# Experts of a mixture over all tokens, against tokens sorted by expert through memory, the steps of fixed places first and of extra places last

## The chip, the core and the metric

The kernel runs on one core of one Trainium2 chip. The metric is the time of one execution on the device in microseconds (us). Three executions of the kernel before took 678.14, 679.23 and 679.41 us; their median is 679.23. The engines are TensorE (PE, with its weight loads as PEld), VectorE (DVE), ScalarE (ACT), GpSimd (POOL) and SyncE (SP), which here only issues transfers. Each of them works through its own queue in the order in which the program wrote it.

## What is computed

The input `x` is 4 batches of 512 tokens with 128 numbers each. Two layers follow:

```
xn = _layernorm(x)
x = x + L0_attn(xn) + L0_ffn(xn)
xn = _layernorm(x)
x = x + L1_attn(xn) + L1_ffn(xn)
```

`L0_attn` is an attention between the channels of 16 heads. `L0_ffn` is the part that changes: a router picks 8 of 64 experts for each token, and each expert is a small gated network with 88 hidden numbers; a shared one of 176 hidden numbers takes every token.

```
expert_out = jax.vmap(lambda gw_, uw_, dw_: _mlp(x, gw_, uw_, dw_))(Wg, Wu, Wd)
routed = jnp.einsum('eth,te->th', expert_out, rw)
shared = _mlp(x, Sg, Su, Sd)
```

Here `_mlp` is `silu(x @ gw.T) * (x @ uw.T) @ dw.T`, and `rw` holds a token's weight for each expert, which is zero for 56 of the 64. `L1_attn` compares each token with the 64 before it, by head, and keeps the 32 nearest of them; `L1_ffn` is a network with ternary weights and 512 hidden numbers. Everything is float32.

## The kernel before

All tokens of a batch stay in SBUF, and every expert is computed for every token; the weights `rw` then remove what was not chosen. The hidden rows of all experts stand behind one another: 2 x 88 shared rows and 64 x 88 routed rows make `NF` = 46 tiles of 128 rows for each batch, so 4 x 46 = 184 steps. A step `n` does this:

- ACT rounds a tile of the weights to float32r (`highs`, tile `Whi`), and POOL takes the remainder (`splits`, tile `Wlo`).
- PE multiplies by the tokens in three products for the gate and three for the up part (`experts`, banks G and U), each 512 columns wide: high by high, high by low, low by high.
- ACT takes the silu (`silus`), DVE multiplies gate and up (`products`, tile S). The routing weights are multiplied in on POOL (`tiles`, `S<-S,Rb`) or on DVE (`weights`, `S<-Rb,bank_G`). To have them by hidden row, PE spreads the router's table with a 0/1 matrix (`spread`).
- PE adds the tile's part of the output into bank A with a float32 matmul of 512 columns (`downs`); the trace has two records for such a matmul.

Only the three small steps of routing (`route`: scores, the best 4 of 8 groups, the best 8 experts), the channel attention (`attend`) and the second layer (`head`, `distances`, `choose`, `gather`, `dense_up`, `dense_down`) stand beside that. `choose` is the selection of the nearest 32: for each of the 8 groups `g` of a batch, DVE runs four rounds of MAX8 and MATCH_REPLACE8 on four tiles.

The order of all this isn't left to a scheduler. Each engine's parts are generators, and `weave` calls them letter by letter from a string in the table `ORDER`; waits between engines are semaphores that the parts set themselves. SP loads all weights once, in about 45 us, and later only stores the output. All these lines are recorded through helpers, so L522, L859, L1345 and L1654 are the lines of the helpers of PE, DVE, ACT and POOL. `S` is a ring of five tiles; free tiles of the second layer (`hf`, `wT` and others) take its place early on.

## Time and profile before

| | us |
|---|---|
| three executions, median | 679.23 |
| the profiled execution, span of its instructions | 676.3 |
| PE busy in it | 638.7 |
| DVE busy | 545.1 |
| ACT busy | 444.6 |
| POOL busy | 365.4 |
| data moved by transfers | 15.81 MB |

The span runs from the first to the last instruction; the 2.9 us between it and the median lie around it, and no row shows them. Busy time is that in which an engine had at least one instruction under way. A matmul's record ends when its last column is through, and the next one starts before that, so the cost of a matmul in a full queue is read from start to start. Issuing a transfer doesn't count as busy; on SP it has a row of its own (SPq).

### The profile page before, as it was taken

The numbers are of one execution on the slowest core, as the hardware profiler recorded it, in microseconds if no ns is written. First come the engines' busy times: TensorE is split into PE (matmuls) and PEld (weight loads), VectorE is DVE, ScalarE is ACT, GpSimd is POOL, SyncE is SP. The second block draws the span as 40 slices with busy tenths as digits, with TensorE's granted clock in tenths as the row PEclk, the third lists the DMA queues.
The fourth block names the chain that finished last, engine by engine and source line by source line (L and its number), as shares of the span: only waits on it lengthen the run. The fifth ranks groups of instructions, "written<-read, shape, count | busy, mean of one in ns | idle before, by whom it ended". The sixth has DMA issues, their size and how long they took to land.

```text
span 676.3 us, 14256 instructions
## 1 busy us (share of the span) xinstructions
PE 638.7 (94%) x4792; PEld 430.7 (64%) x4792; DVE 545.1 (81%) x2461; ACT 444.6 (66%) x802; POOL 365.4 (54%) x448
## 2 busy tenths in 40 slices
PE   4887999999999999999999999999999999998886
PEld 3544766667656666767567567666567776675675
DVE  5987778645975999997976899965485999967997
ACT  3674454646787957448587786455888956467953
POOL 2278366566462787665452886653763576621220
PEclk9999999999999999999999999999999999999999
DMA  8940000000000000000000000000000000000000
GB/s 297 392 131 1 0 1 0 1 0 1 0 1 1 2 2 1 1 1 1 2 0 2 2 1 2 1 1 1 1 1 1 2 1 1 1 1 17 18 18 17
DMA packets 12968, 15.81 MB, mean 23 GB/s; under 512 B 1728, under 2 KB 10832, under 8 KB 12384
## 3 DMA queue, kind: packets, MB, share of 16 engines
q1 hardware_dynamic: 12896, 14.91, 6.3%
q8 instruction: 38, 0.62, 0.4%
q14 instruction: 34, 0.28, 0.1%
HBM read 13.85 MB, written 1.05 MB: 22 GB/s over the span
## 4 chain that ended last, share of the span: by engine, by line
PE 61%; DVE 24%; ACT 7%; POOL 4%; issue 3%; DMA 0%; DVEq 0%; POOLq 0%; ACTq 0%
PE bank_A L522 17%; PE bank_U L522 14%; PE bank_G L522 14%; PE bank_X L522 14%; DVE Wk L1278 6%; DVE m L1275 5%; DVE S L859 4%; DVE GWk L859 2%; POOL PR L1654 2%; ACT L1350 1%; PE bank_X L531 1%; ACT Ed L1345 1%; PE bank_X L825 1%; ACT PR L1345 1%; ACT L1345 1%
## 5 line engine op out<-in xcount | busy, mean ns | idle before, releaser
L1654 POOL TENSOR_TENSOR Wlo<-Wgu,Whi 128x256 fp32r<-128x256 f32 x184 | 134.9, 743 | 119.5 <-ACT Whi L1345 116.5
L522 PE MATMUL bank_A<-S,WdT 128*128 128x512 f32 x346 | 172.2, 599 | 0.2 <-POOL S L1654 0.2
L1654 POOL TENSOR_TENSOR S<-S,Rb 128x512 f32<-128x512 f32 x84 | 108.6, 1294 | 72.0 <-DVE S L859 71.4
L859 DVE TENSOR_TENSOR S<-S,bank_U 128x512 f32<-128x512 f32 x173 | 116.6, 684 | 37.5 <-PE bank_U L522 23.3
L1345 ACT ACTIVATE Whi<-Wgu 128x256 fp32r<-128x256 f32 x184 | 73.0, 413 | 53.0 <-PE bank_U L522 48.5
L522 PE MATMUL bank_G<-xH,Whi 128*128 128x512 f32 x184 | 94.7, 515 | 8.0 <-POOL Wlo L1654 3.8
L522 PE MATMUL bank_U<-xH,Whi 128*128 128x512 f32 x184 | 93.4, 508 | 1.6 <-DVE wT L859 1.1
L522 PEld LDWEIGHTS bank_A<-S,WdT 128*128 128x128 f32 x346 | 61.7, 189 | 34.6 <-issue 21.4
L1278 DVE MATCH_REPLACE8 Wk<-m,Wk 128x79 f32<-128x79 f32 x384 | 82.2, 226 | 0.0
L1345 ACT ACTIVATE bank_G<-bank_G 128x512 f32<-128x512 f32 x83 | 48.4, 583 | 42.9 <-PE bank_G L522 42.6
L1345 ACT ACTIVATE S<-bank_G 128x512 f32<-128x512 f32 x90 | 53.7, 596 | 34.3 <-PE bank_G L522 27.5
L859 DVE TENSOR_TENSOR S<-Rb,bank_G 128x512 f32<-128x512 f32 x83 | 56.4, 680 | 22.5 <-ACT bank_G L1345 17.6
L522 PE MATMUL bank_U<-xH,Wlo 128*128 128x512 f32 x184 | 72.9, 396 | 0.0
L522 PE MATMUL bank_G<-xH,Wlo 128*128 128x512 f32 x184 | 72.9, 396 | 0.0
L522 PE MATMUL bank_G<-xL,Whi 128*128 128x512 f32 x184 | 72.8, 396 | 0.0
L522 PE MATMUL bank_U<-xL,Whi 128*128 128x512 f32 x184 | 72.7, 395 | 0.0
L1275 DVE MAX8 m<-Wk 128x8 f32<-128x79 f32 x384 | 63.9, 228 | 0.0
L522 PEld LDWEIGHTS bank_G<-xH,Whi 128*128 128x128 f32 x184 | 34.7, 189 | 34.7 <-issue 17.2
L522 PEld LDWEIGHTS bank_U<-xH,Whi 128*128 128x128 f32 x184 | 34.7, 189 | 23.8 <-issue 8.9
L1345 ACT ACT_TABLE_LOAD x38 | 48.8, 1283 | 0.7
L1350 ACT ACT_TABLE_LOAD x35 | 44.9, 1283 | 6.5 <-DVE mv L926 4.4
L1654 POOL TENSOR_TENSOR Wk<-Ed,Wk 128x316 f32<-128x316 f32 x31 | 26.8, 863 | 37.1 <-DVE Wk L1278 36.9
(294 smaller groups left out, 1176.0 us busy)
## 6 DMA issues: line engine op xcount, KB each, us to landing
Wgu<-in_Wgu SPq DMA_DIRECT2D x2, 2048.0 KB, 14.4
xs<-in_x SPq DMA_DIRECT2D x4, 256.0 KB, 6.0
wqk<-in_w_qkv SPq DMA_DIRECT2D x1, 1024.0 KB, 6.9
Wgu<-in_Wgu SPq DMA_DIRECT2D x1, 1024.0 KB, 9.5
out<-xs SPq DMA_DIRECT2D x3, 256.0 KB, 2.3
Wgu<-in_Wgu SPq DMA_DIRECT2D x1, 512.0 KB, 4.7
wout<-in_w_out SPq DMA_DIRECT2D x1, 512.0 KB, 8.1
wvT<-in_wvT SPq DMA_DIRECT2D x1, 512.0 KB, 9.2
```

The lines of the kernel that those rows point to most:

```text
L522: return engine.matmul(dst, lhsT, rhs, start=start, stop=stop)
L531: p = engine.transpose(t[0:rows, 128 * i:128 * i + 128], src3[:, i, :], ident)
L825: p = engine.transpose(t[:, 128 * i:128 * i + 128], Wm[s][:, i, :], ident)
L859: return engine.tensor_tensor(dst, a, b, op)
L1275: top[i] = own(engine.max(w8[:, i, 8 * r:8 * r + 8], v[:, i, :]))
L1278: p = engine.match_replace(wk[:, i, :], w8[:, i, 8 * r:8 * r + 8], v[:, i, :], TAKEN)
L1345: return engine.activation(dst, src, f, bias=bias, scale=scale, accum_out=acc)
L1350: engine.preload_act_table_set(LNEXP)
L1654: return engine.tensor_tensor(dst, a, b, op)
```

## The change

The routed experts are no longer computed for all tokens. A batch's tokens are sorted by expert through two tables in HBM, `XS` (inputs) and `YS` (results), each in two copies for even and odd batches.

- Places. Each expert has 64 fixed places (`SLOT`), so 4,096 rows of the table. Tokens beyond the 64th of an expert go to further blocks of 64 places, up to 64 such blocks, the second half of the table. DVE and PE work out each token's place from running counts (bank `rank`, three more PE parts and some 60 more DVE instructions in `route`, 32 of them small ones for the weight of each token's choice) and write it as `rows`; which expert an extra block belongs to goes into `erow`.
- Sending. POOL issues 32 indirect transfers per batch (`sends`), each of which writes 128 tokens of 512 bytes to their places. The tables of inputs are cleared first by two transfers of 4 MB from a zero tile.
- Steps. A batch has 18 steps: 2 shared ones on all tokens, then 16 routed ones of 8 blocks of 64 places. The first 8 routed steps take the fixed places, the last 8 the extra ones, whether these are filled or not. For a routed step, SP loads 512 rows of `XS` (`slots_in`), PE transposes them (4 transposes, `slot_turns`), runs 8 float32 matmuls of 176 columns with 64 stationary columns each, gate and up together (`experts`), ACT takes 2 silus, DVE 2 products of 176 columns, PE transposes back (4, `hidden_turns`), ACT copies, PE runs 8 float32 matmuls of 128 columns (`downs`), ACT copies, SP stores 256 KB to `YS` (`slots_out`).
- Weights. Those of 60 experts stay in SBUF (`WE`, 152 KB each as [128, 304]). Those of 4 more for the fixed places, and those of every extra block, come through a ring of 16 (`RING`), two steps deep: 272 loads of 152 KB, 42 MB in all. The address of an extra block's weights is read from `erow` into registers of SP, four at a time.
- Fetching back. When all 16 steps of a batch are stored, POOL issues 32 indirect reads (`gets`) of 128 rows into a ring of 8 tiles (`LAND`), and DVE adds each to the tokens with its weight (`joins`, 128 in all).
- Gone are the float32r split (`highs`, `splits`), the weights on hidden tiles (`tiles`, `weights`), the spreading (`spread`, `RW`, `Rb`), and the sum through `mo`.
- The table `ORDER` is new for all engines. Products of experts are now float32 throughout.

```diff
-NF = 46
-NR = 44
+SHARED = 2
+QUADS = 16
+STEPS = SHARED + QUADS
+SLOT = 64
+GUD = 2 * NI + C
+ROWS = 2 * NE * SLOT
+KEY = 2.0 ** -14
+RES = 60
+RING = 16
+LAND = 8
...
-        Wgu = sb("Wgu", [128, NF, 256])
-        Whi = [sb(f"Whi{i}", [128, 256], FR) for i in range(WRING)]
-        Wlo = [sb(f"Wlo{i}", [128, 256], FR) for i in range(WRING)]
-        WdT = sb("WdT", [128, NF, 128])
+        WE = sb("WE", [128, RES, GUD])
+        Wr = sb("Wr", [128, RING, GUD])
+        SW = sb("SW", [128, SHARED, 2 * NI])
+        SD = sb("SD", [NI, SHARED, C])
...
+def spill(n):
+
+    return routed(n) % QUADS >= QUADS // 2
+
+
+def quad(n):
+
+    return routed(n) % (QUADS // 2)
+
+
+def slots_of(n):
+
+    return (ROWS // 2 if spill(n) else 0) + 8 * SLOT * quad(n)
...
+            def clear(r):
+
+                sp.wait_ge("zeroed", 1)
+                z4 = Wm[0][:, :, :].rearrange("p a c -> p (a c)").unsqueeze(1).to_broadcast([128, ROWS // 512, 512])
+                load(f"cleared{r}", XS[r].rearrange("(p a r) c -> p a (r c)", p=128, r=4), z4)
...
+            def slots_in():
+                for m in range(B * QUADS):
+                    n = step_of(m)
+                    b = n // STEPS
+                    yield
+                    sp.wait_ge(*scattered(b))
+                    if m >= 2:
+                        sp.wait_ge(full(bank("xt", step_of(m - 2))), nth("xt", step_of(m - 2)) + 1)
+                    load(loaded(m)[0], xq[m % 2][:, :, :],
+                         XS[b % 2][slots_of(n):slots_of(n) + 512, :].rearrange("(j p) c -> p j c", p=128))
+
+            def slots_out():
+                for m in range(B * QUADS):
+                    n = step_of(m)
+                    b = n // STEPS
+                    yield
+                    sp.wait_ge(empty(bank("y", n)), nth("y", n) + 1)
+                    if b >= 2:
+                        sp.wait_ge("joined_y", NT * 8 * (b - 1))
+                    load(f"st_y{m % 2}", YS[b % 2][slots_of(n):slots_of(n) + 512, :].rearrange("(j p) c -> p j c", p=128),
+                         yq[m % 2][:, :, :])
+
+            def weights():
+                owner = list(stream)
+                at = {}
+                for k, (n, t) in enumerate(owner):
+                    b = n // STEPS
+                    yield
+                    e = 8 * quad(n) + t
+                    if k >= RING:
+                        sp.wait_ge("down", owner[k - RING][0] + 1)
+                    if spill(n):
+                        if t % 4 == 0:
+                            sp.wait_ge(empty(bank("rank", b)), nth("rank", b) + 1)
+                            _, at = nc.values_load_multi_w_load_instructions(
+                                erow[0:1, b, e:e + 4], engines=[engine.engine], min_val=0, max_val=(NE - 1) * C,
+                                skip_runtime_bounds_check_because="a count of at most 63 experts, times 128")
+                        src = d["WE"][bass.ds(at[t % 4], C), :]
+                    else:
+                        src = d["WE"][e * C:(e + 1) * C, :]
+                    load(f"ld_r{k % RING}", Wr[:, k % RING, :], src)
...
+            def slot_turns():
+                for m in range(B * QUADS):
+                    n = step_of(m)
+                    yield
+                    t = fill("xt", n)
+                    pe.wait_ge("ld_c", 16)
+                    pe.wait_ge(*loaded(m))
+                    turn4(t, xq[m % 2]).then_inc(sems(full(bank("xt", n))), 1)
+
             def experts():
                 for n in range(total):
-                    b, j, w = n // NF, n % NF, n % WRING
-                    xH, xL = xHs[b % 2], xLs[b % 2]
-                    for key, at in (("g", 0), ("u", 128)):
+                    b, s = n // STEPS, n % STEPS
+                    for k, key in enumerate("gu"):
                         yield
                         t = fill(key, n)
-                        if j == 0:
-                            pe.wait_ge("xL" if b else "xL0", b if b else 1)
-                        pe.wait_ge("wlo", n + 1)
-                        mm(t[:, :], Whi[w][:, at:at + 128], xH[:, :], True, False)
-                        mm(t[:, :], Whi[w][:, at:at + 128], xL[:, :], False, False)
-                        mm(t[:, :], Wlo[w][:, at:at + 128], xH[:, :], False, True).then_inc(
-                            sems(full(bank(key, n))), 1)
+                        if shared(n):
+                            pe.wait_ge(empty(bank("xT", b)), nth("xT", b) + 1)
+                            pe.wait_ge("ld_s", 32)
+                            for i in range(2):
+                                at = 128 * (2 * k + i)
+                                p = mm(t[:, 2 * NI * i:2 * NI * (i + 1)], xTs[b % 2][:, at:at + 128], SW[:, s, :])
+                        else:
+                            pe.wait_ge(empty(bank("xt", n)), nth("xt", n) + 1)
+                            for i in range(2):
+                                for h in range(2):
+                                    at, w = 128 * (2 * k + i) + SLOT * h, 2 * (2 * k + i) + h
+                                    weight_here(pe, n, w)
+                                    p = mm(t[SLOT * h:SLOT * (h + 1), 2 * NI * i:2 * NI * (i + 1)],
+                                           xqT[routed(n) % 2][:, at:at + SLOT], weight(n, w)[:, 0:2 * NI])
+                        p.then_inc(sems(full(bank(key, n))), 1)
...
                     else:
-                        pe.wait_ge(empty(bank("u", m)), nth("u", m) + 1)
-                    mm(T_["A"][:, :], WdT[:, m % NF, :], product_tile(m), m % NF == 0, m % NF == NF - 1).then_inc(
-                        sems("down"), 1)
+                        t = fill("y", n)
+                        pe.wait_ge(empty(bank("ht", n)), nth("ht", n) + 1)
+                        for w in range(8):
+                            i, h = w // 2, w % 2
+                            weight_here(pe, n, w)
+                            p = mm(t[SLOT * h:SLOT * (h + 1), 128 * i:128 * i + 128], hT[:, SLOT * w:SLOT * (w + 1)],
+                                   weight(n, w)[0:NI, 2 * NI:])
+                    p.then_inc(sems("down"), 1)
...
+                t = fill("rank", b)
+                pe.wait_ge("before", 1)
+                pe.wait_ge("marks", b + 1)
+                for j in range(NT):
+                    for i in range(j + 1):
+                        mm(t[:, NE * j:NE * j + NE], before[:, 128:] if i == j else before[:, 0:128],
+                           marks[:, NE * i:NE * i + NE], i == 0, i == j)
+                for i in range(NT):
+                    p = mm(t[0:NE, 320:322], marks[:, NE * i:NE * i + NE], before[:, 0:2], i == 0, i == NT - 1)
+                p.then_inc(sems(full(bank("rank", b))), 1)
+                yield
+                pe.wait_ge("ove", b + 1)
+                mm(ps("rank", b)[:, 384:448], K("ones", NE), ovE[:, :]).then_inc(sems("ovb"), 1)
+                yield
+                pe.wait_ge("ej", b + 1)
+                mm(ps("rank", b)[0:1, 448:512], rk[:, 3:4], ident[0:NE, 0:NE]).then_inc(sems("erow"), 1)
...
             def products():
                 for n in range(total):
-                    s = product_tile(n)
-                    yield
-                    dve.wait_ge(empty(bank("g", n)), nth("g", n) + 1)
-                    t = filled("u", n)
-                    emptied(tt(s, s, t[:, :], ALU.mult), "u", n)
...
+                    for k, key in enumerate("gu"):
                         yield
+                        dve.wait_ge("silu", 2 * n + k + 1)
+                        if n:
+                            dve.wait_ge(full(bank("ht", n - 1)), nth("ht", n - 1) + 1)
+                        t = filled(key, n)
+                        u = t[:, 0:4 * NI].rearrange("p (j w) -> p j w", j=2)[:, :, NI:]
+                        emptied(tt(hs[:, 2 * k:2 * k + 2, :], sg[:, 2 * k:2 * k + 2, :], u, ALU.mult), key, n)
...
+            def joins():
+                for b in range(B):
+                    for q in range(NT * 8):
+                        n, i, k = b * NT * 8 + q, q % NT, q // NT
+                        yield
+                        if q < NT:
+                            dve.wait_ge(empty(bank("ysh", b)), nth("ysh", b) + 1)
+                            dve.wait_ge("wsel", b + 1)
+                        else:
+                            dve.wait_ge("joined_y", n - NT + 1)
+                        dve.wait_ge(f"got{n % LAND}", 16 * (n // LAND + 1))
+                        x = xb(b)[:, i, :]
+                        stt(x, land[:, n % LAND, :], wsel[:, b, i, k:k + 1], x, ALU.mult, ALU.add).then_inc(
+                            sems("joined_y"), 1)
...
-            def split(n):
-                w = n % WRING
-                po.wait_ge("whi", n + 1)
-                tt(Wlo[w][:, :], Wgu[:, n % NF, :], Whi[w][:, :].bitcast(F), ALU.subtract).then_inc(sems("wlo"), 1)
...
+            def sends():
+                for b in range(B):
+                    r = b % 2
+                    for k in range(8):
+                        for i in range(NT):
+                            yield
+                            po.wait_ge("rows", b + 1)
+                            po.wait_ge(f"cleared{r}", 16)
+                            if b >= 2:
+                                for q in range(2):
+                                    po.wait_ge(f"ld_x_{q}", 16 * (QUADS // 2) * (b - 1))
+                            at = 8 * i + k
+                            engine.indirect_dma_start(
+                                out=XS[r], out_offset=bass.IndirectOffsetOnAxis(ap=rows[:, b, at:at + 1], axis=0),
+                                in_=xns[r][:, i, :], in_offset=None).then_inc(sems(scattered(b)[0]), 16)
+
+            def gets():
+                for b in range(B):
+                    for q in range(NT * 8):
+                        n, at = b * NT * 8 + q, 8 * (q % NT) + q // NT
                         yield
-                        s, k = product_tile(n), (n % NF - (NF - NR)) // BLOCK
-                        po.wait_ge(empty(bank("sp", n // NF, k)), nth("sp", n // NF, k) + 1)
-                        po.wait_ge(empty(bank("u", n)), nth("u", n) + 1)
-                        tt(s, s, Rb[k][:, :], ALU.mult).then_inc(sems("tw_p"), 1)
+                        for k in range(2):
+                            po.wait_ge(*stored(k, b))
+                        if n >= LAND:
+                            po.wait_ge("joined_y", n - LAND + 1)
+                        engine.indirect_dma_start(
+                            out=land[:, n % LAND, :], out_offset=None, in_=YS[b % 2],
+                            in_offset=bass.IndirectOffsetOnAxis(ap=rows[:, b, at:at + 1], axis=0)).then_inc(
+                            sems(f"got{n % LAND}"), 16)```

Three places show what the new table and the new parts do to the queues. The first is POOL. Before, a stretch of its queue in the steps of a middle batch, up to where that batch's channel attention (tiles `PR` and `z`) comes in:

```order
L1654 TENSOR_TENSOR S<-S,Rb 128x512 [waits U1_emptied]
L1654 TENSOR_TENSOR Wlo<-Wgu,Whi 128x256 [waits whi] x2
L1654 TENSOR_TENSOR S<-S,Rb 128x512 [waits U1_emptied]
L1654 TENSOR_TENSOR Wlo<-Wgu,Whi 128x256 [waits whi]
L1654 TENSOR_TENSOR PR<-GWk,wqk 128x256 [waits X0_filled,X0_emptied]
```

Now, the same engine from its first sends (`XS<-xn,rows`, batch 0) on; the `PR` and `z` rows are batch 0's attention:

```order
L1810 DMA XS<-xn,rows 8192x128 [waits cleared0,rows]
L1810 DMA XS<-xn,rows 8192x128 x4
L1792 TENSOR_TENSOR PR<-GWk,wqk 128x256 [waits X1_filled,X1_emptied]
L1792 TENSOR_TENSOR PR<-GWk,wqk 128x256 x3
L1810 DMA XS<-xn,rows 8192x128 x3
L1792 TENSOR_TENSOR PR<-PR 128x512 [waits k0]
L1810 DMA XS<-xn,rows 8192x128 [waits pool]
L1810 DMA XS<-xn,rows 8192x128 x2
L1792 TENSOR_TENSOR PR<-PR,z 128x512
```

The attention that batch 0's sends share the queue with is behind or between them; all 32 sends of a batch stand ahead of its first routed step. In the whole queue the order is: sends of batch 0, of batch 1, fetches of batch 0, sends of batch 2, then the sends of batch 3 mixed with the fetches of batch 1 and the second layer of batch 0, and last the fetches of batches 2 and 3.

The second place is SP among the extra steps of batch 0. Before, SP had nothing there: its 42 rows are the loads at the start and the stores of the output. Now (`TENSOR_LOAD erow` reads four addresses, `Wr` is the ring of weights, `ISA` is register work for an address):

```order
L489 DMA YS<-yq 128x4x128 [waits A_emptied]
L489 DMA xq<-XS 128x4x128 [waits U0_filled]
L578 TENSOR_LOAD erow [waits down]
L489 ISA
L489 DMA Wr<-in_WE 128x304
L489 ISA
L489 DMA Wr<-in_WE 128x304
L489 DMA YS<-yq 128x4x128 [waits A_emptied]
L489 ISA
L489 DMA Wr<-in_WE 128x304
L489 ISA
L489 DMA Wr<-in_WE 128x304
```

For each extra step SP now issues 8 loads of weights, a load and a store of places, and 2 reads of addresses, 12 things in one queue, and each waits for what stands ahead of it.

The third place is DVE behind the last product of the last expert step. Before, the last product of batch 3 (`S<-S,bank_U`) had 8 groups of `choose` behind it or next to it; now, after the last product (`hs<-sg,bank_G`), 16 groups follow, those of batch 2 with the joins of batch 3 (`xs<-land,wsel,xs`) between them, then those of batch 3. A piece of it, in the groups of batch 2:

```order
L1421 MAX m<-Wk 128x8 [waits dve] x4
L1424 MATCH_REPLACE Wk<-m,Wk 128x79 [waits dve] x4
L981 SCALAR_TENSOR_TENSOR xs<-land,wsel,xs 128x128 [waits got6,joined_y]
L981 SCALAR_TENSOR_TENSOR xs<-land,wsel,xs 128x128 [waits got7,joined_y]
L1433 TENSOR_REDUCE sm<-m 128x4
L1434 RECIPROCAL sm<-sm 128x4 [waits dve]
L981 SCALAR_TENSOR_TENSOR xs<-land,wsel,xs 128x128 [waits got0,joined_y]
```

So the second layer of batch 2 has moved behind the experts of batch 3.

## Rows read from the trace of the kernel before

**Rows 1.** The page's span and part 1; a window: busy us (count) PE, PEld, DVE, ACT, POOL.

```profile
span 676.3 us, 14256 instructions
...
PE 638.7 (94%) x4792; PEld 430.7 (64%) x4792; DVE 545.1 (81%) x2461; ACT 444.6 (66%) x802; POOL 365.4 (54%) x448
...
90.00:600.00 510.00, 504.26 (x3557) 333.06 (x3556) 418.50 (x1840) 342.07 (x611) 306.56 (x374) 1.00 0.01 1
```

**Rows 2.** Timeline of PE (start, length, instruction), then the chain that ended last.

```profile
138.11 0.39 PE L522 MATMUL bank_G<-xH,Wlo 128*128 128x512 f32 x1
138.34 0.40 PE L522 MATMUL bank_U<-xH,Whi 128*128 128x512 f32 x1
...
139.20 1.72 PE bank_A L522 x4
```

**Rows 3.** Groups by form, POOL: count, busy us, mean ns, idle time before.

```profile
L1654 POOL TENSOR_TENSOR Wlo<-Wgu,Whi 128x256 fp32r<-128x256 f32 x184 | 134.9, 743 | 119.5 <-ACT Whi L1345 116.5 <-DVE hg L867 2.6
L1654 POOL TENSOR_TENSOR S<-S,Rb 128x512 f32<-128x512 f32 x84 | 108.6, 1294 | 72.0 <-DVE S L859 71.4
```

**Rows 4.** The same for DVE.

```profile
L859 DVE TENSOR_TENSOR S<-S,bank_U 128x512 f32<-128x512 f32 x173 | 116.6, 684 | 37.5 <-PE bank_U L522 23.3 <-ACT S L1345 12.1
...
L859 DVE TENSOR_TENSOR S<-Rb,bank_G 128x512 f32<-128x512 f32 x83 | 56.4, 680 | 22.5 <-ACT bank_G L1345 17.6 <-PE bank_A L522 4.8
```

**Rows 5.** The same for ACT.

```profile
L1345 ACT ACTIVATE Whi<-Wgu 128x256 fp32r<-128x256 f32 x184 | 73.0, 413 | 53.0 <-PE bank_U L522 48.5 <-DMA WdT<-in_WdT 1.3
L1345 ACT ACTIVATE S<-bank_G 128x512 f32<-128x512 f32 x90 | 53.7, 596 | 34.3 <-PE bank_G L522 27.5 <-PE bank_A L522 6.4
```

**Rows 6.** Timeline of PE: small float32 matmuls and the row behind each.

```profile
70.02 1.95 PE L522 MATMUL bank_X<-PR,wvT 128*128 128x128 f32 x16
71.81 0.39 PE L522 MATMUL bank_X<-cst,Qb 128*128 128x128 f32 x2
...
242.34 0.60 PE L825 MATMUL bank_X<-cst,Wm 128*128 128x128 f32 x4
242.70 0.48 PE L522 MATMUL bank_G<-xH,Whi 128*128 128x512 f32 x1
...
273.84 1.09 PE L522 MATMUL bank_X<-wout,z 64*64 64x128 f32 x16
274.86 0.50 PE L522 MATMUL bank_G<-xH,Whi 128*128 128x512 f32 x1
```

**Rows 7.** Timeline of SP's issues at the start.

```profile
39.15 0.42 SPq L450 DMA_DIRECT2D hbu<-in_Vb  x1
39.61 0.42 SPq L450 DMA_DIRECT2D dec<-in_dec  x1
```

**Rows 8.** Windows at the start (clock, DMA share, GB/s last); transfers with us to landing.

```profile
20.00:25.00 5.00, 4.78 (x16) 2.59 (x15) 4.60 (x12) 2.43 (x5) 1.49 (x3) 1.00 0.99 417
...
out<-xs SPq DMA_DIRECT2D x3, 256.0 KB, 2.3
...
out<-xs SPq DMA_DIRECT2D x4, 64.0 KB, 1.5
```

**Rows 9.** DVE at the start; POOL on tile PR in a window; POOL.

```profile
26.19 0.21 DVE L1059 MATCH_REPLACE8 wk<-m8r,sfc 128x64 f32<-128x64 f32 x1
...
37.90 1.77 DVE L859 TENSOR_TENSOR yT<-yT,Rb 128x512 f32<-128x512 f32 x1
...
33.00:59.00 26.00, 7.88 (x8) 1.00 0.32 98
...
57.25 1.05 POOL L1654 TENSOR_TENSOR z<-z,rq 128x512 f32<-128x512 f32 x1
```

**Rows 10.** Timeline of DVE, two groups of a selection; the window of the end.

```profile
620.36 0.67 DVE L1275 MAX8 m<-Ed 128x8 f32<-128x79 f32 x4 [2.59 <-ACT Ed L1345]
...
626.40 0.66 DVE L1275 MAX8 m<-Ed 128x8 f32<-128x79 f32 x4
...
600.70:676.30 75.60, 61.55 (x889) 49.04 (x888) 60.58 (x445) 51.80 (x103) 14.24 (x18) 0.96 0.05 16
```

643 lines of the change are left out of this document (322 added, 321 removed).

## The prediction, written before the result

> **What bounds the kernel now.** I read the busy times and a long window first. PE is busy for 638.7 us of the 676.3, and from 90 to 600 us for 504 of 510 [rows 1]; DVE, ACT and POOL have room. So the kernel before is bound by PE's instruction stream up to about 600 us, and then by something else. The timeline of PE gives the price of a step: the float32r products of 512 columns start 0.23 us apart, and two float32 matmuls of the output take 1.72 us, 0.86 each [rows 2]. A step costs 6 x 0.23 + 0.86 = 2.25 us, and 184 of them 414 us. All other work on PE is 638.7 - 414 = 225 us. The last 75.6 us are the second layer of batch 3, from its layer norm on: in it DVE works for 60.6 us, and its selection goes at 6.04 us per group of four tiles, 8 groups in a batch [rows 10].
>
> **What the change does to each engine's total.** *PE.* Four transposes take 0.36 us from their start to the next row's, 0.09 each. Eight matmuls of 128 columns on part of the array (`wout,z`) take 1.02 us, 0.13 each, while on the whole array eight take 1.79 us, 0.22 each [rows 6]. The new matmuls have 64 stationary columns and alternate between the two halves of the bank's partitions, as `wout,z` does, so I take 0.13 for 128 columns and 0.13 x 176/128 = 0.175 for 176. The other end is the whole array's price, 0.22 and 0.31. A routed step is 8 x 0.09 + 8 x 0.175 + 8 x 0.13 = 3.15 us, at most 4.9; 64 of them are 202 us. A shared step is 4 x 0.31 + 4 x 0.09 + 4 x 0.22 = 2.5 us, 8 of them 20. The ranks of routing cost PE about what the spreading did. The sum is 225 + 202 + 20 = 447 us, 190 less than before; with the dear price, 560.
>
> *DVE* loses the products and weights of 512 columns, 116.6 + 56.4 us in the two large groups and some 15 in smaller ones [rows 4]. It gains 144 products of 176 columns (0.68 x 176/512 = 0.24, I take 0.3 with what a short instruction costs; 43 us), 128 joins of 128 columns at 0.25 by the same scaling (0.17 and what a short instruction costs; 32 us), and about 10 us per batch of routing. 545 - 188 + 43 + 32 + 40 = 472 us. *ACT* loses the 73.0 us of `Whi` and about 110 us of silus of 512 columns (184 at 0.6), and gains per routed step three copies of 512 columns at 0.6 and two short silus, 2.4 us [rows 5]: 444.6 - 183 + 64 x 2.4 + 10 = 425 us. *POOL* loses 134.9 and 108.6 [rows 3] and about 16 smaller ones, which leaves 106 us, and gains 256 indirect transfers at a price P that no row of this trace shows. *SP* goes from 42 rows to 734.
>
> So no engine is full any more by its total, and what decides is the chain: places of batch 0, its sends, four batches of steps, the end.
>
> **The chain, stage by stage.** (a) *Places of batch 0.* Now the best 8 are marked at 26.4 us [rows 9]. Counting, ranks and places add some 20 small instructions and four changes of engine, about 7 us: 33 us.
>
> (b) *Sends.* All 32 stand ahead of the first load of places, and batch 0's attention stands between them on POOL: 7.9 us on `PR` and three more of 1.05 [rows 9], 11 us. P is bounded from below by what SP needs for an issue, 0.47 us from start to start [rows 7], and from above by 2.3 us, the landing of 256 KB; 64 KB landed in 1.5 [rows 8]. A send has a list to read and 128 rows to write, so it should be nearer to the landing of the same 64 KB than to a plain issue; I take 1.2. 32 x 1.2 + 11 + 2.3 for the first load, and 1.5 of `xl`: 53 us, so the first routed step begins near 86 us. In the order, PE has until then only routing, attention and shared steps, some 45 us of its 225.
>
> By the Trainium skill, "DMA: Bandwidth & Descriptors", section "Anatomy of one DMA — SWDGE (gpsimd) path", a GpSimd transfer costs about 2.0 us, of which most is the receipt of the last write and little is the making of descriptors. By it POOL would be held much shorter than 1.2 us; were it held for SP's 0.47 [rows 7], this stage would be 23 us shorter and the time 608. No run here shows a transfer from GpSimd.
>
> (c) *A batch of 16 steps.* PE's other work is 225 less the 45 ahead, 62 in the last 75.6 us [rows 10], and about 30 for the second layer of batch 2, which the new order puts behind the experts: 88 us, 22 per batch. The fixed half is bound by PE: 8 x 3.15 + 2 x 2.5 + 11 = 41 us. The extra half isn't. There SP issues 10 transfers per step, 10 x 0.47 = 4.7 us [rows 7], and two reads of addresses. Such a read is in no row; it can cost nothing beside an issue, or as much as a small transfer's 1.5 us [rows 8]; I take 1 us, so SP needs 6.7 us. The ring holds only two steps, and a step's weights can be asked for only when the step two before has finished, which hides none of the landings; I add 0.8 and take 7.5 us per extra step. The transfers themselves fit: 1.25 MB of weights, 0.5 of places and about 0.3 of sends or fetches are 2 MB, at the 417 GB/s of the start [rows 8] 5 us. So the extra half is 60 us, a batch 101, four 404 us. The bounds: with SP free, PE sets 41 + 36 = 77 us per batch, 308 in all; with 1.5 us per read and no overlap of the landing (2.3), 10 us per step and 121 per batch.
>
> Hidden under that, with its price if the cover goes: POOL must run 192 sends and fetches, 68 us of attention and second layer, from 33 us until batch 3's sends are done, 33 + 192 x 1.2 + 68 = 331 us, while batch 3's steps are due at 86 + 303 = 389. The cover is 58 us, gone at P = 1.5.
>
> (d) *The end.* Behind the last product stand the second layers of batches 2 and 3. Batch 2: 8 x 6.04 for its groups, 32 joins of batch 3 (8 us), and its `gather` 6 us, together 62. The fetches of batch 3 go meanwhile: 32 x 1.2 and 14 us for the groups' weights, 52, hidden. Then batch 3's second layer as now, 75.6. Together 138 us.
>
> The sum is 86 + 404 + 138 = 628 us of span. The profiled span of before is 676.3, and the median 679.23 lies 2.9 above it; so the time is **631 us**, 7% faster.
>
> **Rivals.** *A: POOL is the bound, and it is slower.* Each 0.1 us on P above 1.2 adds 3.2 us in (b), above 1.5 also 19 in (c), and above 1.5 about 3 in (d). For 48 us more (to 679): 0.3 x 32 = 10, then 38 at 25 per 0.1, so the point is P = 1.65; at P = 1.9 the time is 631 + 10 + 4 x 25, about 741. For it speaks that DVE and POOL already hold each other up: a DVE product of two tiles in SBUF took 1.77 us [rows 9] where one with an operand in a bank takes 0.68 [rows 4], and sends write while DVE is busy. Against it: POOL has no data to work through in a send. The Trainium skill, "SBUF — State Buffer", section "Who interferes with whom", says that DVE's two-port copies lock GpSimd out so that it cannot write descriptors; that rule makes P larger than it is alone, and this rival likelier. Chance 0.15.
>
> *B: the extra steps cost over 9 us each, and it is slower.* They are 32; 48 us more is 1.5 us each, 9.0 in place of 7.5. A read of addresses of 1.7 us does it, or the landing of each step's weights in the open, as in the upper bound of (c): 631 + 80 = 711. For it: the ring of two steps, and one queue in which loads of places wait behind loads of weights. Against it: transfers have landed while others were issued in the start. Chance 0.15.
>
> *C: SP hides behind PE.* Reads are near nothing, issues overlap PE's work: 308 us for the batches in place of 404, so 535 in all; half of the way, 583. Chance 0.15. *D: the gain on PE is eaten by matmuls at the whole array's price*, 1.7 us more in each fixed step (in the extra ones SP still covers it), 54 us: 685, a little slower. Chance 0.04, with the pairs in [rows 6] against it.
>
> **Numbers.** My forecast, 600 to 665 us, has 0.51. Faster by over 0.2% (less than which a measurement of this kernel can't tell from no change): 0.51 + C 0.15 + a share of A, B and D that stays under 678, 0.02: 0.68. Same 0.02. Slower 0.30. The range that holds 8 in 10 leaves out the best of C and the worst of A and B: 570 to 715 us; the forecast's own range is 600 to 665.
>
> **What the profile would show.** PE busy near 450 us. The first load of `xq` near 84 us, and `XS<-xn` issues on POOL 1.2 us apart. Extra steps 7.5 us apart with PE waiting for `Wr`, SP's queue full in them; fixed steps 5 us apart. The last product (`hs`) near 490 us, and 138 us behind it in which DVE is busy. The prediction is wrong if POOL's queue is full from 33 us to the end (A), if extra steps come over 9 us apart (B), or under 6 (C).

## The result, and the profile after

On the first occasion the changed kernel took 823.12 us (median of 4 runs, 821.74 to 825.49) against 679.32 us of before: 1.2109 times as long, interval 1.2078 to 1.214. I had predicted 631, with a range of 570 to 715. The page of that execution, and the answers to [rows 3 to 5] (this and all further groups: line, engine, output and input, count, then busy us, mean ns, and the idle time before):

```profile
span 821.1 us, 18063 instructions
...
PE 605.7 (74%) x6064; PEld 446.5 (54%) x6064; DVE 475.8 (58%) x2788; ACT 379.2 (46%) x728; POOL 361.6 (44%) x405
...
PEclk9995656988979976976689877789959998756985
...
L1810 POOL DMA_INDIRECT XS<-xn,rows x128 | 126.4, 988 | 75.5 <-issue 43.5
L1823 POOL DMA_INDIRECT land<-YS,rows x128 | 123.8, 967 | 77.5 <-issue 40.5
L973 DVE TENSOR_TENSOR hs<-sg,bank_G 128x176 f32<-128x176 f32 x144 | 47.1, 333 | 127.8 <-ACT sg L1493 54.1
```

No engine is full, as expected, and DVE (472 expected) and POOL (106 and 256 transfers) are where the sums had them; ACT is 46 us under its 425. PE is 159 us above its 447, at a mean granted clock of 0.807 where before had 0.996.

The same kernel, unchanged, took 818.02 us on a second occasion and **683.67 us on a third** (677.54 to 690.74, 5 runs; before 679.17 beside it; ratio 1.0027, interval 0.9945 to 1.0108). Six near copies of it, below, lie between 684.63 and 690.64 us. The kernel before, too, has one slow execution on record, 906.92 us at a mean clock of 0.66, among 25 with a median of 679.24. So two things have to be explained: some 139 us (823 less 684) that came with the occasion, and the 53 us between 631 and 684. The page of the third occasion, then the windows between its stages (first the first routed step of batch 0, then the beginning of its extra half, and so on to the last product; columns as in [rows 8]: length, busy us of PE, its weight loads, DVE, ACT, POOL, then clock, DMA share, GB/s):

```profile
span 681.9 us, 18063 instructions
...
PE 540.6 (79%) x6064; PEld 401.2 (59%) x6064; DVE 478.1 (70%) x2788; ACT 380.5 (56%) x728; POOL 361.0 (53%) x405
```

```profile
0.00:105.60 105.60, 63.84 (x275) 45.54 (x275) 60.84 (x294) 18.05 (x31) 52.14 (x63) 0.85 0.74 250
105.60:132.20 26.60, 25.82 (x278) 19.77 (x278) 14.41 (x75) 18.11 (x37) 17.75 (x18) 0.88 0.73 215
132.20:194.40 62.20, 59.62 (x579) 43.84 (x577) 37.14 (x135) 37.52 (x74) 32.47 (x36) 1.00 0.83 241
194.40:239.60 45.20, 40.12 (x361) 30.78 (x360) 32.34 (x158) 23.59 (x49) 30.90 (x36) 0.92 0.51 143
239.60:310.90 71.30, 60.49 (x661) 43.52 (x660) 45.40 (x238) 47.76 (x94) 48.96 (x50) 0.95 0.77 225
310.90:348.80 37.90, 36.23 (x524) 28.44 (x522) 30.05 (x196) 30.03 (x58) 26.79 (x31) 1.00 0.63 181
348.80:427.40 78.60, 61.55 (x731) 43.50 (x729) 49.46 (x285) 53.59 (x97) 46.59 (x52) 0.89 0.74 214
427.40:467.40 40.00, 37.65 (x570) 30.15 (x568) 38.12 (x253) 32.70 (x65) 25.68 (x29) 1.00 0.61 170
467.40:528.30 60.90, 50.94 (x643) 35.38 (x642) 45.93 (x261) 43.00 (x81) 21.05 (x26) 0.97 0.79 225
528.30:606.00 77.70, 53.36 (x771) 43.66 (x769) 65.94 (x467) 39.25 (x70) 45.12 (x53) 0.76 0.16 43
606.00:681.90 75.90, 51.02 (x696) 36.60 (x695) 58.49 (x436) 36.86 (x78) 13.56 (x17) 0.75 0.03 8
```

Added up, with the same cuts in the first trace (115.8, 152.7, 225.2, 278.5, 377.6, 434.7, 532.9, 581, 650 us), in us:

| stage | predicted | first occasion | third |
|---|---|---|---|
| up to the first routed step | 86 | 115.8 | 105.6 |
| four fixed halves | 164 | 195.4 | 149.7 |
| four extra halves | 240 | 338.8 | 273.0 |
| behind the last product | 138 | 171.1 | 153.6 |
| span | 628 | 821.1 | 681.9 |

In the eight windows of the batches of the third occasion PE is busy for 372 of 422.7 us, 88%. There it is the engine nearest to full, as before the change (99%, [rows 1]).

### The profile page after: what moved, and what is told of

Its sections match the earlier page's. It is cut to its first block and busy times, and to the rows that moved or that the text cites. A ratio compares the mean times of both kernels' runs of the same rounds, so it can differ in the third digit from the quotient of the medians.

```text
span 821.1 us, 18063 instructions
## 1 busy us (share of the span) xinstructions
PE 605.7 (74%) x6064; PEld 446.5 (54%) x6064; DVE 475.8 (58%) x2788; ACT 379.2 (46%) x728; POOL 361.6 (44%) x405
## 5 line engine op out<-in xcount | busy, mean ns | idle before, releaser
L1810 POOL DMA_INDIRECT XS<-xn,rows x128 | 126.4, 988 | 75.5 <-issue 43.5
L1823 POOL DMA_INDIRECT land<-YS,rows x128 | 123.8, 967 | 77.5 <-issue 40.5
L973 DVE TENSOR_TENSOR hs<-sg,bank_G 128x176 f32<-128x176 f32 x144 | 47.1, 333 | 127.8 <-ACT sg L1493 54.1
L1493 ACT ACTIVATE sg<-bank_G 128x176 f32<-128x176 f32 x144 | 44.9, 317 | 95.7 <-PE bank_G L612 54.6
L1424 DVE MATCH_REPLACE8 Wk<-m,Wk 128x79 f32<-128x79 f32 x384 | 82.4, 228 | 0.0
L612 PE MATMUL bank_G<-Wr,xqT 128*64 128x176 f32 x544 | 76.0, 370 | 7.0 <-issue 4.2
L1792 POOL TENSOR_TENSOR Wk<-Ed,Wk 128x316 f32<-128x316 f32 x31 | 26.8, 863 | 95.0 <-DVE Wk L1424 94.3
L1493 ACT ACTIVATE hT<-bank_U 88x512 f32<-88x512 f32 x72 | 42.6, 591 | 55.4 <-PE bank_U L621 28.0
L1421 DVE MAX8 m<-Wk 128x8 f32<-128x79 f32 x384 | 64.1, 229 | 0.5 <-DVE m L1421 0.5
L621 PE MATMUL bank_U<-cst,xq 128*128 128x128 f32 x256 | 50.9, 333 | 16.8 <-DMA xq<-XS 8.9
L612 PE MATMUL bank_A<-Wr,hT 88*64 88x128 f32 x544 | 50.4, 327 | 13.6 <-ACT hT L1493 6.2
L612 PEld LDWEIGHTS bank_G<-Wr,xqT 128*64 128x64 f32 x544 | 44.0, 157 | 29.9 <-issue 17.7
L612 PE MATMUL bank_G<-WE,xqT 128*64 128x176 f32 x480 | 55.3, 361 | 6.6 <-DVE hs L973 4.2
L621 PE MATMUL bank_U<-cst,hs 128*88 128x128 f32 x288 | 52.6, 313 | 9.4 <-DVE hs L973 8.8
L1493 ACT ACTIVATE yq<-bank_A 128x512 f32<-128x512 f32 x64 | 38.1, 595 | 41.0 <-PE bank_A L612 22.4
L1493 ACT ACTIVATE xqT<-bank_U 128x512 f32<-128x512 f32 x64 | 38.1, 595 | 38.1 <-PE bank_U L621 22.2
L621 PEld LDWEIGHTS bank_U<-cst,xq 128*128 128x128 f32 x256 | 35.7, 169 | 30.8 <-issue 23.3
L612 PEld LDWEIGHTS bank_A<-Wr,hT 88*64 88x64 f32 x544 | 38.8, 165 | 24.4 <-issue 21.3
L621 PEld LDWEIGHTS bank_U<-cst,hs 128*88 128x88 f32 x288 | 33.5, 138 | 25.2 <-issue 17.7
L612 PE MATMUL bank_A<-WE,hT 88*64 88x128 f32 x480 | 36.6, 290 | 12.6 <-ACT hT L1493 8.9
L612 PEld LDWEIGHTS bank_G<-WE,xqT 128*64 128x64 f32 x480 | 35.2, 154 | 19.7 <-issue 11.5
L981 DVE SCALAR_TENSOR_TENSOR xs<-land,wsel,xs 128x128 f32<-128x128 f32 x128 | 44.9, 379 | 0.3 <-DMA land<-YS,rows 0.2
## 6 DMA issues: line engine op xcount, KB each, us to landing
xq<-XS SPq DMA_DIRECT2D x64, 256.0 KB
YS<-yq SPq DMA_DIRECT2D x64, 256.0 KB
xs<-in_x SPq DMA_DIRECT2D x4, 256.0 KB, 11.4
```

The lines of the kernel that those rows point to most:

```text
L612: return engine.matmul(dst, lhsT, rhs, start=start, stop=stop)
L621: p = engine.transpose(t[0:rows, 128 * i:128 * i + 128], src3[:, i, :], ident)
L973: return engine.tensor_tensor(dst, a, b, op)
L981: return engine.scalar_tensor_tensor(dst, a, s, b, op0, op1, accum_out=acc)
L1421: top[i] = own(engine.max(w8[:, i, 8 * r:8 * r + 8], v[:, i, :]))
L1424: p = engine.match_replace(wk[:, i, :], w8[:, i, 8 * r:8 * r + 8], v[:, i, :], TAKEN)
```

## Experiments 1: 139 us that belong to the occasion

In the first trace I saw stretches like this one. PE's timeline (start, length, instruction, in brackets the idle time before it and its releaser), POOL's, and ACT's:

```profile
347.17 0.34 PE L612 MATMUL bank_X<-mk,wqk 32*32 32x79 f32 x4 [0.28 <-issue]
348.60 0.30 PE L612 MATMUL bank_X<-mk,wqk 32*32 32x79 f32 x3 [1.08 <-issue]
350.05 0.34 PE L612 MATMUL bank_X<-mk,wqk 32*32 32x79 f32 x3 [1.16 <-issue]
...
357.43 1.27 PE L612 MATMUL bank_X<-mk,wqk 32*32 32x79 f32 x32
```

```profile
347.66 0.96 POOL L1810 DMA_INDIRECT XS<-xn,rows  x1 [0.31 <-issue]
348.93 0.96 POOL L1810 DMA_INDIRECT XS<-xn,rows  x1 [0.30 <-issue]
...
352.72 0.96 POOL L1810 DMA_INDIRECT XS<-xn,rows  x1 [0.30 <-issue]
```

```profile
347.57 0.46 ACT L1493 ACTIVATE Ra<-Pk 16x316 fp32r<-16x316 f32 x1
355.76 0.60 ACT L1493 ACTIVATE yq<-bank_A 128x512 f32<-128x512 f32 x1 [7.73 <-remote]
```

The 32 small matmuls of one group of distances took 1.27 us at 357.4 and over 9 us at 346.4, some three at a time with up to 1.2 us between them, and nothing in the program for them to wait for. Meanwhile POOL sent back to back. ACT waited too: the record of the product that fills its input in `bank_A` ends at 346.2 (1.09 us from 345.07), but that product's semaphore rises at 355.74, and ACT starts at 355.76. Over the trace PE has 53.7 us of such idle time ("issue"), 46 of them in pauses that overlap an indirect transfer of POOL; ACT has 28 us of it and 110 of waits for which the trace shows no releaser, DVE 38 and 52. I call them standstills. On the second occasion they are there again: PE 53.9 us in 64 pauses where the first had 61, and 38 of the first's 53.7 us lie within four instructions of a pause of the second. On the third PE has none, ACT 1.1, DVE 4.2.

Two more things set the first two traces apart from the third, both counted in their records of semaphores. A semaphore that a PE instruction raises does so 0.015 us behind the instruction's end (median of all three); 0.5 to 15 us behind it rose 123 and 115 times on the first two occasions, 4 times on the third. So signals came late as well, and waits without a releaser, such as ACT's above, can be waits for such a signal. And records are missing: 9,978 and 10,079 rises are recorded, 14,712 on the third. The transfers themselves took no longer: those of SP filled the DMA engines for 40.7% of 821.1 us and 48.9% of 681.9, 334 and 333 us, and those that load instructions for 0.5% and 0.7%, 4 and 5 us.

**Three variants that I first read wrongly.** Before I ran the kernel again, I had run three variants (their results stand in the next sections), and all were far under 823 us and without standstills on PE. I took this for the effect of their edits, then repeated the changed kernel.

> The changed kernel once more, unchanged, on the chip on which the runs to be compared with it run. In its first trace PE, ACT and DVE stand still for some 54, 27 and 38 us with nothing to wait for, PE always beside an indirect transfer of POOL, and 160 us of waits on ACT and DVE have no releaser in the trace; in the three variants run so far (same transfers on POOL in two of them) PE has less than 1 us of such time. If the program itself does this, the time is again 823 us and the standstills are there. If it was the chip or the run, the time is lower, 730 to 760 us, and the gains of the first three variants were too large by as much.

818.02 us, with the standstills. So it seemed to be the program itself, and I asked how little of a change removes them. With 16 matmuls of 256 columns added in the first two routed steps:

> As e2, but with filler in the first two routed steps only: 16 matmuls, 2 us of PE in all, and the rest of the program as in the changed kernel, moved by 16 instructions. If the standstills of the changed kernel belong to its logic, they are still there and the time is 815 to 825 us. If they belong to the image of the program (any shift of it changes them), they can be gone: then the time is that of the change without them, somewhere from 720 to 770 us, and the gains of the other variants have to be counted from there.

690.64 us, none. Then one PE instruction (its edit follows), one POOL instruction, one tensor in memory with a store into it at the very end, one DVE instruction:

```diff
+                    if m == 0:
+                        pe.wait_ge("before", 1)
+                        mm(t[0:2, 0:2], before[:, 0:2], before[:, 0:2])
```

> The changed kernel with one PE instruction more (a float32r matmul of 2 by 2 ahead of the first routed step). If the standstills hang on where PE's instructions lie, they vanish and the time is 685 to 700 us, as with 16 added matmuls; if they hang on another engine's or on memory, it stays at 815 to 825 us.

> The changed kernel with one POOL instruction more (a part of a tile of zeros set once before, at 10 us, ahead of all transfers), PE's, ACT's and DVE's programs untouched. If the standstills hang on POOL's program, they vanish, 685 to 700 us; if on PE's alone, 815 to 825 us.

> The changed kernel with a spare tensor of 64 KB in memory declared ahead of the places and results, and one store into it at the very end of SP's program. It moves the scratch tensors in memory and no instruction ahead of the end. If the standstills come from where the sends write, they change: any time from 685 to 825 us. If they hang on the instructions of the engines alone, 815 to 825 us.

> The changed kernel with one DVE instruction more (a small copy done twice at the start), PE's, ACT's and POOL's programs untouched. If any shift of the image does, 685 to 700 us; if only PE's or POOL's own, 815 to 825 us.

688.12, 684.63, 684.63 and 686.56 us; ratios to before 1.0135, 1.0063, 1.0086 and 1.0075, each within 0.005. All four can't be the cure, which left the suspicion that it was none of them. So the kernel itself and a copy that differs in one constant ran on one chip:

> The changed kernel unchanged, for the third time. If the standstills belong to its image, 815 to 825 us again; if they belonged to the chips of the first two occasions, 680 to 700 us like all variants with one instruction more.

> The changed kernel with one constant changed (the 1e-20 that guards a sum of weights against zero is 2e-20): the same instructions in the same places. If the standstills hang on the layout of the image, it is as slow as the changed kernel; if 680 to 700 us beside a changed kernel of 820, not even the layout is the cause.

683.67 and 685.56 us. That settles it: neither the logic of the change nor the layout of its program is enough to make the standstills, since the same program runs with them and without. What does is open. The chip of the second occasion was another one than those of the third and of all variants of the changed kernel. It ran the kernel before in its usual 678.86 us. It also ran b1 below, whose 128 indirect transfers start 3.2 us apart (median), with 0.2 us of standstill on PE. But b1 has the other two signs in small: 17 of PE's rises in its batches come 0.5 to 1.4 us late, and some 300 of about 6,870 records are missing, while b2 and b3 on the same chip, without indirect transfers, show neither. So the signs go with POOL's indirect transfers on that chip. What holds the engines up, the chip, the moment, or the recording of the profile itself (every execution has a clock on record, and where engines stood still records were lost), no run tells apart.

How 54 us become 139: PE's busy time is 605.7 against 540.6, 65 more, for the same 6064 instructions at a clock of 0.807 in place of 0.892; its standstills are 54 and 0; the rest of its idle time (waits for DVE, ACT, DMA and POOL, in which their standstills and late signals lie) is 161.7 and 141.3. 65 + 54 + 20 = 139, all that lies between the spans. Which of the 65 are the clock alone, no run shows.

## Experiments 2: PE's clock

A clock of 0.81 is a cost in itself, and it could have come from PE's pauses. So I filled them.

```diff
+            def warm(t, count):
+                for _ in range(count):
+                    mm(t[:, 0:256], before[:, 0:128], before[:, :])
...
                     t = fill("xt", n)
+                    pe.wait_ge("before", 1)
+                    warm(t, WARM)
                     pe.wait_ge("ld_c", 16)
```

> The changed kernel with idle work added on PE: ahead of each wait for places, for gate and up inputs and for hidden values of a routed step, two float32r matmuls of 256 columns into the bank that the step overwrites next, 8 per step, 512 in all, 0.11 us each at the full clock, 56 us of PE. If PE's clock (0.81 on the average, against 1.00 before) is what the change costs, and it falls because PE now stands still so often, the granted clock rises to over 0.9 in the batches, PE's own rows shorten, and the time falls to 760 to 800 us. If the clock has another cause, or PE's busy time isn't on the path, it is slower, up to 823 + 56 = 880 us.

> As the run with 512 float32r matmuls of 256 columns (e2), but each has 2 stationary and 2 moving columns: as many instructions in the same places, next to no work. e2 took the time from 818 to 734 us and also took away PE's 54 us of standstill beside POOL's transfers, so it doesn't tell the two apart. If the gain came from the work that kept PE's clock up (0.81 to 0.88), it is gone here: 810 us or more. If it came from the standstills, which depend on where the instructions lie in the program and not on what they do, PE has again almost none and the time is 710 to 760 us, with the clock near 0.81.

733.91 us with the wide filler, clock 0.884; 701.01 with the narrow one, clock 0.907; without any, 684 and 0.892. Against 823 the filler looked like a gain of 89 us; against the right base it costs 50, about its own 56 us, and the clock didn't rise. The 512 empty instructions cost 17, the work in the others 33 more. The windows say why little was to be had: in the batches the clock was already 0.88 to 1.00, and it is low where PE hardly matters, 0.75 in the last 75.9 us, which are as long as the 75.6 of before at 0.96 [rows 10]. What the wide filler does show is who bounds the batches: with 56 us more of work for PE in the routed steps they took 476.6 us in place of 421.8.

## Experiments 3: the stream of weights, and POOL's transfers

```diff
-            return WE[:, 8 * quad(n) + t, :]
+            return WE[:, min(8 * quad(n) + t, RES - 1), :]
```

(and the loads of the extra steps skipped in SP's queue)

> The changed kernel without the streaming of weights in the extra halves: the 8 extra steps of a batch multiply with the resident weights of the step with the same number in the fixed half, so tokens beyond an expert's 64 places get another expert's matrices. 256 loads of 76 KB and the 64 reads of addresses on SP are gone; every step, send, fetch and product stays. If the extra half is bound by SP and its ring of two steps, as the prediction had it, the extra steps fall from 8.5, 12.3, 11.4 and 7.8 us (in the four batches) to the 5 to 6.7 us of the fixed ones, 32 x 4.5 = 145 us less, 680 us. If they are bound by PE at its lower clock and by engines that wait for each other in the written order, little changes, less than 40 us: 785 us or more.

```diff
                         for i in range(NT):
                             yield
+                            if k >= KEEP:
+                                continue
```

(and the same for fetches and joins)

> The changed kernel with only the first four of a token's eight experts sent, fetched and joined: 64 sends and 64 fetches on POOL and 64 joins on DVE less; all steps still run, on half empty places, so the output lacks half of the experts' shares. POOL has 128 x 1.28 = 164 us less to do. If POOL's queue and what its indirect transfers do to the other engines bound the kernel, the first step starts 20 us earlier (98 in place of 116 us) and the time falls by 60 us or more. If PE, the clock and the written order bound it, the start gains at most 20 us and the rest little: 795 us or more. In the trace, all of PE's 54 us of idle time ahead of which nothing is to be waited for lie beside an indirect transfer; if these cause them, they halve to some 27 us.

676.31 and 675.69 us; against 684, some 8 us each. Both numbers hit what the expectation gave to "SP" or "POOL bounds it", for the wrong reason: the 139 us of the occasion were in the base. (The loads that e1 leaves out are of 152 KB each, not 76.) The windows of e1 answer the question by themselves. Its four extra halves, with no weight streamed:

```profile
135.20:196.30 61.10, 58.11 (x578) 44.33 (x576) 35.25 (x129) 37.35 (x74) 31.87 (x36) 0.94 0.36 107
...
243.00:307.30 64.30, 55.48 (x660) 42.24 (x658) 44.23 (x231) 47.41 (x93) 47.05 (x48) 0.95 0.39 113
...
344.60:419.10 74.50, 58.20 (x732) 41.82 (x729) 49.58 (x285) 53.42 (x97) 46.84 (x52) 0.91 0.38 108
...
456.20:518.00 61.80, 51.68 (x663) 37.47 (x662) 47.94 (x286) 42.29 (x82) 25.33 (x30) 0.92 0.34 94
```

61.1, 64.3, 74.5 and 61.8, where the kernel with the stream has 62.2, 71.3, 78.6 and 60.9: 11 us less in all. PE is busy for 223 of their 262 us.

The stages of e3 say where its 8 us come from. With 16 sends per batch the first load of places goes out 20.7 us earlier (96.11 in the changed kernel), and the first routed step starts no earlier (105.59). SP, then PE:

```profile
75.42 0.93 SPq L490 DMA_DIRECT2D xq<-XS  x2
```

```profile
106.18 1.11 PE L622 MATMUL bank_U<-cst,xq 128*128 128x128 f32 x4
```

From there to the last product it is 420.7 us against 421.8, and behind it 147.7 against 154.5. So half of the transfers gained nothing at the start or in the batches; the gain lies behind the last product, where the joins stand in DVE's queue.

> The variant with resident weights in the extra halves (e1) and the one with four of eight experts sent, fetched and joined (e3) in one kernel; the output lacks the same as theirs together. Each alone took the time from 684 to 676 us. If SP's stream and POOL's transfers covered for each other, both gone give far more than 16 us, down to 600 to 640. If PE, at a mean clock of 0.89, and the chain of four engines in the written order bound it, 655 to 672 us.

661.4 us (657.87 to 664.94). Twice 8 would have been 668, no further off than the two runs lie apart, so it isn't shown that the two cover for each other. PE with the order around it keeps the rest, as the second case said.

On the kernel before, which is bound by PE and has no routing through memory, the price of a transfer can be seen by itself:

```diff
                     split(n)
+                    if 40 <= n < 168:
+                        po.wait_ge("rows", 1)
+                        engine.indirect_dma_start(
+                            out=XS[n % 8], out_offset=bass.IndirectOffsetOnAxis(ap=rows[:, 0:1], axis=0),
+                            in_=cst[:, 0:128], in_offset=None).then_inc(sems(f"extra{n % 8}"), 16)
```

> The kernel before with 128 indirect transfers added on POOL, one behind each second half of weights of steps 40 to 167: 128 rows of 512 bytes from SBUF to a scratch tensor in memory, like the sends of the changed kernel, read by nobody. POOL gets 128 x 1.28 = 164 us more work and had 311 us of room. If an indirect transfer keeps PE from issuing (54 us beside 256 transfers, 0.2 us each, or up to 1 us in the worst stretches), the PE-bound kernel gets slower by 27 us or more beyond what the busy POOL of its sister run b2 costs; if not, it is within 5 us of it.

> The kernel before with the same amount of work on POOL in the same places, but as arithmetic: two additions of 256 columns, some 0.65 us each, in place of each of the 128 indirect transfers. It shows what POOL's lateness alone costs: from nothing to 20 us, if the ring of split weights can't cover 1.3 us at each step.

> The kernel before with the same 128 transfers of 64 KB into memory issued by SP as plain transfers at the same points. If the movement of data as such (not POOL's part in it) disturbed the other engines, it would be slower here too; expected is no change, 679 us within 3.

733.61, 780.99 and 679.31 us. POOL's groups in b1 and b2:

```profile
L1679 POOL DMA_INDIRECT XS<-cst,rows x128 | 129.8, 1014 | 20.6 <-issue 18.9
```

```profile
L1656 POOL TENSOR_TENSOR busy<-cst 128x256 f32<-128x256 f32 x256 | 189.4, 740 | 10.0
```

The data themselves cost nothing (b3). What costs is the time POOL is held: 150 us in b1 for 55 us more, 199 in b2 for 102. My first case for b1, slower than b2, is refuted, and so is my price for b2, at most 20 us. POOL's 54% of before [rows 1] wasn't room that could be filled: the `Wlo` products and the tiles of `S` stand in the same queue, and in b2 PE waits 12.9 and 17.9 us for them. Its pauses also go with a lower clock, 0.952 in place of 0.996: 37 of b2's 102 us are PE's own rows, 675.7 against 638.7.

## Experiments 4: the written order

> The changed kernel with one thing else in POOL's order: the 32 sends of batch 0 stand ahead of all pieces of its attention, where 5 of them stood ahead of the first. The sends then end near 29.4 + 32 x 1.28 = 71 us in place of 95, and the attention of batch 0 waits for that, 33 us later than now. If the start is bound by POOL's queue, the first routed step begins earlier than its 105.6 us and the time falls by up to 20 us. If it is bound by PE's order, in which the attention of batch 0 and parts of that of batch 1 stand ahead of the first routed step, that step begins later, 120 to 140 us, and the time rises by 10 to 30 us.

725.38 us. The sends end earlier and the first load of places goes out at 80.3 us in place of 96.1, but PE waits 44 us for the first piece of the attention, and its first routed step comes last in that row. SP, then PE:

```profile
80.29 0.93 SPq L489 DMA_DIRECT2D xq<-XS  x2
```

```profile
81.92 1.98 PE L612 MATMUL bank_X<-PR,cst 128*64 128x512 f32 x4 [44.38 <-POOL PR L1792]
...
144.76 1.11 PE L621 MATMUL bank_U<-cst,xq 128*128 128x128 f32 x4
```

39 us later at the first routed step (105.6 in the changed kernel) are 39 us more in the span (681.9 to 721.0). That is more than the 10 to 30 expected. Nothing later takes it up, and the start is bound by the attention that stands ahead of that step in PE's order: delaying that attention costs (n8), and halving the sends gains nothing (e3).

> The changed kernel with the same pieces of work on every engine in another written order, made by taking at each free moment of an engine the most urgent piece whose inputs are there, by the durations in the trace; one wait is added (the first dense layer behind the last attention, since both use PR). Nothing is removed: all sends, fetches, streamed weights and clears stay. If what the change costs is transfers, SP and POOL themselves, little changes: 780 us or more. If it is that engines wait for each other in the written order (DVE, ACT and POOL are busy for 58, 46 and 44% only), it takes 60 to 140 us off: 680 to 760 us.

764.08 us, without standstills, with the kernel of e7 at 690.64 on the same chip. So 73 us worse, and the second case is refuted in its sign: an order made from the durations of one trace is no better than the one written. That the order matters is shown by it, and by n8; a better one wasn't found.

## Why the prediction was wrong

The prediction of 631 us was wrong twice over, and by different steps.

**What no step held: the standstills, 139 us of the 192.** The price of a send or fetch, in (b) and in rival A, was the time that POOL is held and nothing on the others. On the occasion of the result PE stood still for 53.7 us, most of it beside such transfers, its rows took 65 us more at a lower clock, and other waits 20 us more. Whether the transfers are the cause stays open. On a third occasion none of this was there, and the time was 684: inside the range of 570 to 715, outside the forecast of 600 to 665. No row of before could show this, as it has no indirect transfer.

**(a) and (b), 86 us, was 105.6.** The step that failed is that the sends decide when the first routed step begins. The places were ready earlier (first send at 29.4, not 33), P measured 1.28 us (0.97 of transfer and 0.30 between), not 1.2. The group of the third occasion:

```profile
L1810 POOL DMA_INDIRECT XS<-xn,rows x128 | 126.7, 990 | 70.6 <-issue 47.6 <-DVE rows L978 17.7 <-DMA xq<-XS 3.9
```

The Trainium skill ("DMA: Bandwidth & Descriptors", section "Anatomy of one DMA — SWDGE (gpsimd) path") has the making of descriptors as the small part of a transfer; by this row a transfer, whatever part of it that is, holds POOL for 0.99 us, more than an issue of SP's 0.47 [rows 7]. The size of P was right, its use wasn't. The sum took POOL's queue as full, while it also waits for other engines in the attention, and the first load went out at 96.1 us. But the load isn't what PE's first step waited for longest: in e3 it went out at 75.4, and the step began at 106.2 all the same. PE's order decides: parts of batch 1's attention and of the setup stand ahead of the step, and PE is full in the last window, at a clock of 0.68:

```profile
96.10:105.60 9.50, 9.07 (x44) 7.18 (x42) 1.94 (x5) 0.60 (x1) 4.75 (x6) 0.68 0.27 79
```

The term that hid this is that PE has "until then only routing, attention and shared steps, some 45 us of its 225"; it was busy for 63.8 and waited for DVE, ACT and POOL in between, and the setup was among it.

**(c), 404 us, was 422.7: near in size by luck, wrong in cause.** The step that failed is that the extra half is bound by SP. A read of addresses takes 0.30 us, not 1; the row of the third occasion (minimum, median, maximum in ns):

```profile
L578 SPq TENSOR_LOAD <-erow x64: 295/300/713, 97.1 to 521.4; - x64
```

With the whole stream gone (e1) the extra halves lose 11 of 273 us. PE is busy in them for 232.6 us, and more work for PE makes the batches longer nearly by as much (e2). I had spread PE's other 22 us per batch evenly, while the order lays most of it (attention of the next batches, second layer of earlier ones) into the extra halves: they hold 2614 of PE's instructions, the fixed halves 1733, for as many steps. So the fixed halves came out shorter than 41 (37.4 on the average), the extra ones longer than 60 (68.3), and the sum fitted. At full clock the prices of the small matmuls held: in the piece below, from the start of each row to the next one's, four of 176 columns (8 passes) take 0.75 us, 0.19 each where 0.175 was taken, and eight of 128 columns (16 passes) 0.93, 0.12 each where 0.13 was taken. Only the transposes are dearer, 0.44 and 0.53 for four, where 0.36 was taken [rows 6]. A routed step is 3.4 us by these, where 3.15 was taken, 16 us more for 64 of them:

```profile
168.67 0.60 PE L621 MATMUL bank_U<-cst,xq 128*128 128x128 f32 x4
169.11 0.60 PE L621 MATMUL bank_U<-cst,hs 128*88 128x128 f32 x4
169.64 0.82 PE L612 MATMUL bank_G<-Wr,xqT 128*64 128x176 f32 x8
170.39 1.12 PE L612 MATMUL bank_X<-wqk,Gs 128*128 128x512 f32 x2
171.44 1.09 PE L612 MATMUL bank_A<-Wr,hT 88*64 88x128 f32 x16
172.37 1.05 PE L612 MATMUL bank_G<-Wr,xqT 128*64 128x176 f32 x8
```

So PE's total of 447 failed by the clock. 0.892 on the average is 1.2 GHz for 21.6% of 681.9 us, 147 us; at PE's mean busy share of 79% that is 116 us at half the speed, 58 us lost (worked out, not measured). With it and the 16 us, 447 becomes 521 of the 540.6; the other 20 are open.

**(d), 138 us, was 153.6.** The last 75.9 us are as predicted (75.6). Batch 2's second layer took 77.7 in place of 62; DVE's work in it, 65.9 us, was nearly right (the 32 joins took 11.9 us where 8 were taken), but it isn't full there: it is idle for 11.8 us, 7.2 of them in one wait for ACT's `Ed`.

**Rivals.** A (POOL bounds): P stayed under 1.65, no send or fetch held POOL for more than 1.42 us on the first or third occasion, and halving the transfers gave 8 us; refuted off the bad occasion. Its price of 25 us per 0.1 counted the first sends twice: the 192 transfers behind the 19 us hold the 32 of (b). B (extra steps over 9 us): on the first occasion 338.8 / 32 = 10.6 us each, but not by reads or the ring. On the third 8.5. C fell because PE has more work, though its premise, SP hidden, was the right one. D: the prices held.

## What to carry to other kernels

When a result is far from every case, run the same program again elsewhere before explaining it, and run the unchanged kernel beside each set of variants: three of my readings were off by 139 us until I did. Look too at whether the trace is whole: those of the first two occasions lacked a third of their records of semaphores. A saving in total busy time (PE 638.7 to 540.6 us here) is worth nothing where the chain around it, start 105.6 and end 153.6 us, is added in series; ask for each stage which engine's order ends it. Spread other work over a loop as the order lays it, not evenly, or the bound of each half is misread. And the first wait that looks long isn't the bound until a run takes it away: with half of the sends the first step began no earlier.

## What the runs showed of the hardware

- The same program, with stretches of indirect transfers of POOL one per 1.28 us, ran on two occasions with standstills of PE, ACT and DVE of up to some 9 us (54 us in all on PE), semaphores that rose late 123 and 115 times, and a third of the records of rises missing, and on others without. The cause is open.
- An indirect transfer of 128 rows of 512 bytes holds POOL for 0.97 us, with 0.30 to the next one (1.01 us in b1); on a PE-bound kernel 128 of them cost 55 us, the same bytes sent by SP nothing.
- 512 filler matmuls in PE's pauses left the granted clock where it was (0.884 and 0.907 against 0.892).
- Two address reads and eight loads per step, from a register's address, held SP for so little that taking away all 256 loads was worth 8 us.
